# Second MLP product from two fp16 halves, and the work of the slot shared anew between GpSimd, ScalarE and VectorE

## Chip, cores, metric

One core of a Trainium2 chip. The time is that of one execution on the device, in microseconds (us); three runs of each kernel are taken and the median is quoted.

## What is computed

The input x has 4 sequences of 2048 rows of 256 numbers, fp32. Two sublayers are applied, each wrapped as x + layernorm(f(layernorm(x))). Only the second is touched by the change; its f has two layers:

```python
x = x + layernorm(attn(layernorm(x)))            # softmax over the columns, one head
x = x + layernorm(ffn(layernorm(x)))
# ffn: two layers, each
h = shift_token(x)                               # right half of a row comes from the row before
q, k, v = split(h @ wqkv, 3)                     # 8 heads of 64
q, k = rotary(l2norm(q) * qs), rotary(l2norm(k) * ks)
x = x + local_attention(q, k, v) @ wo            # windows of 128 rows, own window and the one before
h = layernorm(shift_token(x)) * lg + lb
a, g = split(h @ w1 + b1, 2)                     # HID = 682 columns each
x = x + (a * gelu(g)) @ w2 + b2
```

## The kernel before

`phase_a` computes the first sublayer and stores its rows; `phase_b` computes the second. `phase_b` first prepares the weights in a block of its own (lines 519 to 646): it splits `wqkv`, `wo` and `w1` into a high and a low part, scales `w1` by a power of two so that both parts fit fp16, folds the scale of `w1` back through `w2` (L608), and scales the rotary tables (L578). This block ends when the slowest engine is done, and the pipeline starts after it.

The pipeline works on windows of 128 rows: 64 per layer, 128 in all. A **slot** `s` is one turn of every engine's `run(s, r, pairs, layer)`, with `r = s % 4`. The order of work on each engine is written out by hand in `run`, and engines meet at semaphores only; each engine runs its queue strictly in order. In slot `s`, TensorE does in turn: the transposes of q and k of window s-1 (L812, L819); the products of window s with `wqkv`, first q, then k, then v (L834), where v waits for `qT_lo`; the transposes of the attention weights of window s-2 (L850); its product with v (L862), which waits pair by pair for the copies `probsT` by ScalarE; the scores of window s-1 (L875); the product with `wo` (L888); the transpose of the next input (L801). Then comes the MLP, for two windows at a time: in an **even slot** the first MLP product, 66 fp16 matmuls (L909), in an **odd slot** the second, `hid` times `w2` in fp32 (L920), which also waits until three heads' scores have left bank 3. Every fourth slot the loop jumps back (`slots`), so every second even slot is the first after a jump.

The other engines in a slot:

- ScalarE: copies qT and kT (L939, L942); the squares of q and of k (L946, L948); the copy of v (L951); four copies `probsT` (L957); the copy oT (L960); eight exponentials (L967); the copy hT (L932); in even slots six gelus (L980). In an even slot the exp and gelu tables are loaded in turn.
- VectorE: qT_low and kT_low (L1063, L1065); in even slots `layer_output`, two additions (L1028); the statistics of the MLP input (L1072 to L1076, the last gives `var2`); the rotation of q in three products (L1006 to L1008); the normalised MLP input `xh` and its fp16 copy (L1082, L1085); the rotation of k; in odd slots of layer 2 the statistics of the output (L1035 to L1040); oT_low (L1055); the eight masked scores (L1103), with `ss_min` (L1015) ahead of the last pair; eight normalisations of the weights, with a reciprocal ahead of each pair (L1113, L1116), between them xp and hT_low; in odd slots of layer 2 the output's normalisation (L1049); in even slots six products `hid` (L1139).
- GpSimd: `rstd2` from `var2` (L1165); the sums of squares in six halvings (L1155), two of them here and four after qr; the low half of `xh` (L1170); the sums qr and kr (L1174, L1177); in odd slots of layer 2 `rstdf`; the power -1/2 of 16 norms, `rn` (L1188); k times its norm, `kr` (L1193); `xb` (L1199); in odd slots of layer 2 `fin` (L1205).
- SyncE starts the DMAs; each of its waits stands in front of what it queues later. The transposing DMA of `xh_hl` (L778) waits for `xh_hi` and `xh_lo`.

## Time and profile before

| | us |
|---|---|
| three runs | 3128.81, 3130.56, 3132.86 (median 3130.56) |
| the profiled execution | 3132.01 |
| its span in the trace | 3130.2 |
| phase A and the weights, until the pipeline starts | 0 to 722.8 |
| pipeline | 722.8 to 3130.2 |

In the text T is the start of an odd slot and U that of an even one, both counted from TensorE's first transpose of q (L812); "U+6.8" is 6.8 us after it. A busy time is the time in which at least one instruction of the group ran; matmuls overlap one another, so that starts, not durations, give their pace. A row's last bracket is the idle time of the engine just before it and what ended it. "Layer 1" and "layer 2" are the two layers of the second sublayer (`layer` 0 and 1 in the code).

### The profile page before, as it was taken

The page shows a single profiled execution, that of the slowest core. Times are in us where ns is not written, and L with a number is a line of the kernel's source. Part 1 is how long each engine was busy: PE and PEld are TensorE (multiplying, and loading weights), DVE is VectorE, ACT ScalarE, POOL GpSimd, SP SyncE. Part 2 cuts the span into 40 slices and gives each one's busy share as a digit, 9 for nine tenths or more (in the row PEclk, how much of TensorE's full clock was granted, in tenths as well). Part 3 has the DMA queues.
Part 4 walks back from the last instruction along what each step waited for, and adds up shares of the span by engine and source line. Part 5 has one row for each costly group of instructions (what it writes and reads, how often), then busy time and mean ns, then how long its engine had stood idle before and what let it go on. Part 6 is the DMA issues. An engine that isn't in the chain of part 4 may idle for free.

```text
span 3130.2 us, 79769 instructions
## 1 busy us (share of the span) xinstructions
...
## 2 busy tenths in 40 slices
...
DMA packets 273326, 177.65 MB, mean 57 GB/s; under 512 B 95758, under 2 KB 271090, under 8 KB 272754
## 3 DMA queue, kind: packets, MB, share of 16 engines
...
## 4 chain that ended last, share of the span: by engine, by line
PE 74%; POOL 1%; issue 1%; DVE 0%; ACT 0%; DMA 0%; POOLq 0%; SPq 0%; DVEq 0%; ACTq 0%
PE b_ps L834 17%; PE b_ps L909 15%; PE b_ps L920 10%; PE b_ps L862 8%; PE b_ps L850 7%; PE b_ps L888 6%; PE b_ps L875 6%; PE b_ps L819 2%; PE b_ps L812 2%; PE b_ps L801 1%; POOL b_sq L1155 0%; POOL b_rn L1188 0%; POOL b_t L1177 0%; POOL b_kr L1193 0%; DVE b_probs L1103 0%
## 5 line engine op out<-in xcount | busy, mean ns | idle before, releaser
L967 ACT ACTIVATE b_probs<-b_probs,b_negmax 128x256 f32<-128x256 f32 x1024 | 505.9, 496 | 78.3 <-DVE b_negmax L1103 77.4
L834 PE MATMUL b_ps<-b_wqkv,b_hT_hi 128*128 128x512 f32 x1536 | 494.6, 403 | 1.0 <-DVE b_hT_lo L991 1.0
L909 PE MATMUL b_ps<-b_h2T,b_w 128*128 128x256 f16 x4224 | 474.1, 273 | 6.4 <-DMA b_h2T<-b_xh_hl 6.4
L909 PEld LDWEIGHTS b_ps<-b_h2T,b_w 128*128 128x128 f16 x4224 | 414.3, 98 | 55.2 <-DMA b_h2T<-b_xh_hl 6.8
L1155 POOL TENSOR_TENSOR b_sq<-b_sq 128x512 f32<-128x512 f32 (+5 forms) x768 | 418.9, 545 | 64.8 <-ACT b_sq L948 24.7
L1188 POOL TENSOR_TENSOR b_rn<-b_ss_min,b_mhalf 128x16 f32<-128x16 f32 x128 | 377.4, 2949 | 109.9 <-DVE b_ss_min L1015 109.7
L1116 DVE TENSOR_SCALAR b_probs<-b_probs,b_rinv 128x256 f32<-128x256 f32 x1024 | 409.6, 442 | 18.2
L1165 POOL TENSOR_TENSOR b_rstd<-b_var,b_mhalf 128x1 f32<-128x1 f32 x128 | 72.1, 564 | 552.0 <-DVE b_var L1076 552.0
L417 PE MATMUL a_ps<-a_xn_hl,a_E 128*128 128x256 f16 x3072 | 344.5, 273 | 8.8 <-DVE a_E L293 8.8
L920 PE MATMUL b_ps<-b_w,b_hid 128*128 128x256 f32 x1536 | 342.2, 379 | 1.2 <-DVE b_hid L1139 1.2
L417 PEld LDWEIGHTS a_ps<-a_xn_hl,a_E 128*128 128x128 f16 x3072 | 299.4, 98 | 44.2 <-ACT a_e L366 9.6
L834 PEld LDWEIGHTS b_ps<-b_wqkv,b_hT_hi 128*128 128x128 f32 x1536 | 284.8, 192 | 55.2 <-ACT b_hT_hi L932 1.4
L1103 DVE CUSTOM_DVE_ANT_0 b_probs<-b_ps,b_mask,b_rn 128x256 f32<-128x256 f32 x768 | 324.5, 479 | 0.0
L920 PEld LDWEIGHTS b_ps<-b_w,b_hid 128*128 128x128 f32 x1536 | 286.8, 190 | 37.9 <-DVE b_hid L1139 1.5
L834 PE MATMUL b_ps<-b_wqkv,b_hT_lo 128*128 128x512 f32 x768 | 304.6, 397 | 0.0
L957 ACT COPY b_probsT<-b_ps 128x512 f32<-128x512 f32 x512 | 264.0, 610 | 4.7 <-PE b_ps L850 4.6
L980 ACT ACTIVATE b_gl<-b_ps,b_b,b_w_unit 128x256 f32<-128x256 f32 (+1 forms) x384 | 203.1, 562 | 101.3 <-DVE b_hid L1139 69.1
L862 PE MATMUL b_ps<-b_probsT,b_v 128*64 128x128 f32 x4096 | 251.9, 276 | 0.0
L850 PEld LDWEIGHTS b_ps<-b_ident_f,b_probs 128*128 128x128 f32 x2048 | 232.7, 142 | 20.0 <-DVE b_xpp L1028 2.5
L850 PE MATMUL b_ps<-b_ident_f,b_probs 128*128 128x128 f32 x2048 | 245.9, 273 | 3.5 <-DVE b_xpp L1028 2.2
L862 PEld LDWEIGHTS b_ps<-b_probsT,b_v 128*64 128x64 f32 x4096 | 220.9, 137 | 21.5 <-ACT b_probsT L957 18.1
L1139 DVE SCALAR_TENSOR_TENSOR b_hid<-b_ps,b_b1a,b_gl 128x256 f32<-128x256 f32 (+1 forms) x384 | 177.0, 478 | 53.2 <-ACT b_gl L980 46.7
...
## 6 DMA issues: line engine op xcount, KB each, us to landing
b_hx<-xs_dram SPq DMA_DIRECT2D x256, 64.0 KB, 1.9
b_rot<-rot_dram SPq DMA_DIRECT2D x128, 128.0 KB, 2.1
b_xr<-xs_dram SPq DMA_DIRECT2D x128, 128.0 KB, 2.1
xp_dram<-b_xp SPq DMA_DIRECT2D x128, 128.0 KB, 1.7
b_h<-xp_dram SPq DMA_DIRECT2D x256, 64.0 KB, 1.8
...
```

Of the source, the lines that this page charges most:

```text
L417: last = nc.tensor.matmul(ps[:, bank, 0:D], E[:, j, a, i * P:(i + 1) * P], xn_hl[:, b % 2, j, c, :], start=(j == 0 and a == 0 and c == 0), ...
L834: last = nc.tensor.matmul(ps[:, bank, :], hT[:, k, :], wqkv[:, ds(layer(s), 1), part, k, bank * INNER:(bank + 1) * INNER], start=(k == 0 a ...
L850: last = nc.tensor.transpose(ps[:, 3 + p, n * P:(n + 1) * P], probs[:, 2 * p + n // 2, (n % 2) * P:(n % 2 + 1) * P], ident_f[:])
L862: last = nc.tensor.matmul(ps[h * DH:(h + 1) * DH, 7, p * P:(p + 1) * P], v[:, window, (2 * p + h) * DH:(2 * p + h + 1) * DH], probsT[:, p, ...
L909: last = nc.tensor.matmul(ps[:, bank, half * 2 * P:(half + 1) * 2 * P], w1[:, ds(layer(2 * j), 1), wp, k, first:first + P], h2T[:, hp, k, ...
L920: last = nc.tensor.matmul(ps[:, 3, n * D:(n + 1) * D], hid[:, c, n * P:(n + 1) * P], w2[:, ds(layer(2 * j), 1), c, :], start=(c == 0), sto ...
L957: nc.scalar.copy(probsT[:, p, :], ps[:, 3 + p, :]).then_inc(pT_kept, 1)
L967: nc.scalar.activation(probs[:, h, :], probs[:, h, :], ACT.Exp, bias=negmax[:, h:h + 1], scale=-1.0, accum_out=rowsum[:, h:h + 1]).then_in ...
L1103: nc.vector.tensor_tensor_reduce(probs[:, h, :], head_scores(h), which, rn[:, (r - 1) % 2, h:h + 1], ABOVE_ALL, ALU.add, ALU.min, negmax[: ...
L1116: nc.vector.tensor_scalar(probs[:, h, :], probs[:, h, :], rinv[:, h:h + 1], None, ALU.mult).then_inc(probs_ready, 1)
L1155: nc.gpsimd.tensor_tensor(target, target, sq[:, :, width:2 * width], ALU.add).then_inc(ss_halved, 1)
L1188: nc.gpsimd.tensor_tensor(rn[:, r % 2, :], ss_min[:], mhalf[:], ALU.pow).then_inc(rn_ready, 1)
```

## The change

In the steady part, the second MLP product takes three fp16 products (high by high, high by low, low by high) in place of one fp32 product; GpSimd splits `hid` into the halves `hid_hl`, four of the six blocks at the end of an even slot and two in the odd slot behind `rstd2` and `shift2`. Its unit is restored in `layer_output`. ScalarE makes `xh` and its fp16 copy from `rstd2` and a new `shift2`, between the squares and `probsT`, and copies v behind `probsT`. The sum of squares is one halving on GpSimd and a reduction on VectorE (`sum_squares`), which stands ahead of the output's statistics. The norms of k and of q are raised to the power apart, k's first. A rotation is two products, and one reciprocal serves four heads. The semaphore counts follow (three terms become two).

```diff
@@ ... steady part
-        pe.wait_ge(hid_ready, HC * (j + 1))
+        pe.wait_ge(hid_lo, HC * (j + 1))
         if in_range(s - 1):
             pe.wait_ge(scores_kept, HEADS * (s - 1) + BANK_READ[3])
         for n in range(2):
             for c in range(HC):
-                last = nc.tensor.matmul(ps[:, 3, n * D:(n + 1) * D], hid[:, c, n * P:(n + 1) * P], w2[:, ds(layer(2 * j), 1), c, :],
-                                        start=(c == 0), stop=(c == HC - 1))
+                for a, (hp, wp) in enumerate(PARTS):
+                    last = nc.tensor.matmul(ps[:, 3, n * D:(n + 1) * D], hid_hl[:, hp, c, n * P:(n + 1) * P],
+                                            w2[:, ds(layer(2 * j), 1), wp, c, :],
+                                            start=(c == 0 and a == 0), stop=(c == HC - 1 and a == 2))
         last.then_inc(w2_done, 1)
...
-        act.wait_ge(v_done, s + 1)
-        wait(act, pv_done, s - 2)
-        nc.scalar.copy(v[:, r, :], ps[:, 2, :]).then_inc(v_kept, 1)
+    t = s - 3
+    if in_range(t):
+        act.wait_ge(shift2_ready, t + 1)
+        wait(act, xh_lo, t)
+        nc.scalar.activation(xh[:], h2[:, (r - 3) % 2, :], ACT.Identity, bias=shift2[:], scale=rstd2[:]).then_inc(xh_ready, 1)
+        wait(act, h2T_loaded, 16 * t)
+        nc.scalar.activation(xh_hl[:, 0, :], h2[:, (r - 3) % 2, :], ACT.Identity, bias=shift2[:], scale=rstd2[:]).then_inc(xh_hi, 1)
     t = s - 2
     if in_range(t):
         wait(act, pv_done, t)
         for p in range(HP):
             act.wait_ge(pT_done, HP * t + p + 1)
             nc.scalar.copy(probsT[:, p, :], ps[:, 3 + p, :]).then_inc(pT_kept, 1)
+    if in_range(s):
+        act.wait_ge(v_done, s + 1)
+        wait(act, pv_done, s - 2)
+        nc.scalar.copy(v[:, r, :], ps[:, 2, :]).then_inc(v_kept, 1)
+    if in_range(t):
         act.wait_ge(pv_done, t + 1)
         wait(act, wo_done, t)
+        nc.vector.tensor_tensor(by_half(t2[:, n, :]), by_half(ps[:, n, :])[:, :, ::-1, :],
+                                factor(2 * n + 1).rearrange("p h (c d) -> p h c d", c=2), ALU.mult).then_inc(terms, 1)
...
         wait(dve, rn_ready, s)
-        nc.vector.tensor_scalar(ss_min[:], sq[:, :, 0], 1e-24, None, ALU.max).then_inc(ss_ready, 1)
+        nc.vector.tensor_scalar(ss_min[:], ss[:], 1e-24, None, ALU.max).then_inc(ss_ready, 1)
+def sum_squares(s):
+    if in_range(s):
...
+        nc.vector.tensor_reduce(ss[:], sq[:, :, 0:DH // 2], AX.X, ALU.add).then_inc(ss_summed, 1)
+def norm_stats(s, r):
+    t = s - 3
+    if in_range(t):
+        dve.wait_ge(h2_loaded, 32 * (t + 1))
+        nc.vector.bn_stats(st2[:], h2[:, (r - 3) % 2, :]).then_inc(st2_ready, 1)
+        wait(dve, shift2_ready, t)
+        wait_apart(dve, st2_ready, t + 1, passed_dve)
+        nc.vector.bn_aggr(mv2[:], st2[:]).then_inc(mv2_ready, 1)
+        dve.wait_ge(mv2_ready, t + 1)
+        nc.vector.tensor_scalar(var2[:], mv2[:, 1:2], EPS, None, ALU.add).then_inc(var2_ready, 1)
+        nc.vector.tensor_scalar(negmean2[:], mv2[:, 0:1], -1.0, None, ALU.mult).then_inc(negmean2_ready, 1)
 def layer_output(j, r, layer):
...
+                                           ALU.mult, ALU.add).then_inc(xpp_ready, 1)
 def output_stats(j, r, layer):
...
     layer_output(pairs - 3, r, layer)
...
-        wait_apart(dve, st2_ready, t + 1, passed_dve)
-        nc.vector.bn_aggr(mv2[:], st2[:]).then_inc(mv2_ready, 1)
-        dve.wait_ge(mv2_ready, t + 1)
-        nc.vector.tensor_scalar(var2[:], mv2[:, 1:2], EPS, None, ALU.add).then_inc(var2_ready, 1)
+    norm_stats(s, r)
     rotate(s, r, 0, q_sq, q_terms, qr_ready)
-    t = s - 3
-    if in_range(t):
-        dve.wait_ge(rstd2_ready, t + 1)
-        wait(dve, xh_lo, t)
-        nc.vector.tensor_scalar(xh[:], h2[:, (r - 3) % 2, :], mv2[:, 0:1], rstd2[:], ALU.subtract, ALU.mult).then_inc(xh_ready, 1)
-        dve.wait_ge(xh_ready, t + 1)
-        wait(dve, h2T_loaded, 16 * t)
-        nc.vector.tensor_copy(xh_hl[:, 0, :], xh[:]).then_inc(xh_hi, 1)
     rotate(s, r, 1, k_sq, k_terms, kr_ready)
+    sum_squares(s)
     output_stats(pairs - 3, r, layer)
...
-            nc.vector.reciprocal(rinv[:, 2 * p:2 * p + 2], rowsum[:, 2 * p:2 * p + 2]).then_inc(rinv_ready, 1)
-            dve.wait_ge(rinv_ready, HP * t + p + 1)
+            if p % 2 == 0:
+                dve.wait_ge(exp_done, HEADS * t + 2 * p + 4)
+                nc.vector.reciprocal(rinv[:, 2 * p:2 * p + 4], rowsum[:, 2 * p:2 * p + 4]).then_inc(rinv_ready, 1)
+                dve.wait_ge(rinv_ready, 2 * t + p // 2 + 1)
...
+        wait(dve, hid_lo, HC * j)
...
-def halve(s, first, end):
-    if in_range(s):
-        pool.wait_ge(k_sq, s + 1)
-        for n in range(first, end):
-            width = DH >> (n + 1)
-            target = sq[:, :, 0:width]
-            wait(pool, ss_halved, HALVINGS * s + n)
-            nc.gpsimd.tensor_tensor(target, target, sq[:, :, width:2 * width], ALU.add).then_inc(ss_halved, 1)
+def hid_halves(j, first, end):
+    if in_range(2 * j):
+        wait(pool, w2_done, j)
+        for c in range(first, end):
+            rows = slice(0, P if c < FULL else REST)
+            wait_apart(pool, hid_ready, HC * j + c + 1, passed_pool)
+            nc.gpsimd.tensor_copy(hid_hl[rows, 0, c, :], hid[rows, c, :]).then_inc(hid_hi, 1)
+            pool.wait_ge(hid_hi, HC * j + c + 1)
+            nc.gpsimd.tensor_tensor(hid_hl[rows, 1, c, :], hid[rows, c, :], hid_hl[rows, 0, c, :], ALU.subtract).then_inc(hid_lo, 1)
...
     if in_range(t):
         pool.wait_ge(var2_ready, t + 1)
+        wait(pool, xh_hi, t)
         nc.gpsimd.tensor_tensor(rstd2[:], var2[:], mhalf[:, 0:1], ALU.pow).then_inc(rstd2_ready, 1)
-    halve(s, 0, 2)
-    if in_range(t):
+        pool.wait_ge(negmean2_ready, t + 1)
+        pool.wait_ge(rstd2_ready, t + 1)
+        nc.gpsimd.tensor_tensor(shift2[:], negmean2[:], rstd2[:], ALU.mult).then_inc(shift2_ready, 1)
+    if r % 2 == 1:
+        hid_halves(pairs - 2, HID_EARLY, HC)
+    if in_range(s):
+        pool.wait_ge(k_sq, s + 1)
+        nc.gpsimd.tensor_tensor(sq[:, :, 0:DH // 2], sq[:, :, 0:DH // 2], sq[:, :, DH // 2:DH], ALU.add).then_inc(ss_halved, 1)
+    t = s - 3
+    if in_range(t):
+        pool.wait_ge(xh_ready, t + 1)
         pool.wait_ge(xh_hi, t + 1)
         wait(pool, h2T_loaded, 16 * t)
         nc.gpsimd.tensor_tensor(xh_hl[:, 1, :], xh[:], xh_hl[:, 0, :], ALU.subtract).then_inc(xh_lo, 1)
     if in_range(s):
-        pool.wait_ge(q_terms, 3 * (s + 1))
+        pool.wait_ge(q_terms, 2 * (s + 1))
         wait(pool, qT_done, s)
         nc.gpsimd.tensor_tensor(qr[:], t1[:, 0, :], t2[:, 0, :], ALU.add).then_inc(qr_ready, 1)
-        halve(s, 2, HALVINGS)
-        pool.wait_ge(k_terms, 3 * (s + 1))
+        pool.wait_ge(k_terms, 2 * (s + 1))
         nc.gpsimd.tensor_tensor(t1[:, 1, :], t1[:, 1, :], t2[:, 1, :], ALU.add).then_inc(kr_sum, 1)
...
-        wait(pool, scores_kept, HEADS * (s - 1))
-        nc.gpsimd.tensor_tensor(rn[:, r % 2, :], ss_min[:], mhalf[:], ALU.pow).then_inc(rn_ready, 1)
-    if in_range(s):
-        pool.wait_ge(rn_ready, s + 1)
+        nc.gpsimd.tensor_tensor(rn_k[:], ss_min[:, HEADS:2 * HEADS], mhalf[:, 0:HEADS], ALU.pow).then_inc(rnk_ready, 1)
+        pool.wait_ge(rnk_ready, s + 1)
         pool.wait_ge(kr_sum, s + 1)
         wait(pool, kT_done, s)
         nc.gpsimd.tensor_tensor(by_head(kr[:]), by_head(t1[:, 1, :]),
-                                rn[:, r % 2, HEADS:2 * HEADS].unsqueeze(2).to_broadcast([P, HEADS, DH]), ALU.mult).then_inc(kr_ready, 1)
+                                rn_k[:].unsqueeze(2).to_broadcast([P, HEADS, DH]), ALU.mult).then_inc(kr_ready, 1)
+        wait(pool, scores_kept, HEADS * (s - 1))
+        nc.gpsimd.tensor_tensor(rn[:, r % 2, :], ss_min[:, 0:HEADS], mhalf[:, 0:HEADS], ALU.pow).then_inc(rn_ready, 1)
     t = s - 2
     if in_range(t):
         pool.wait_ge(xp_ready, t + 1)
         wait(pool, xpp_ready, t - 3)
         nc.gpsimd.tensor_tensor(xb[:, (r - 2) % 4, :], xp[:, r % 2, :], b2[:, ds(layer(t), 1), :], ALU.add).then_inc(xb_ready, 1)
```

While the weights are prepared, `w2` is scaled and split, the first columns of `w1` (those of a) take a scale that bounds `hid`, and the loads of `w2` and `b1` stand ahead of those of the rotary tables and `wqkv`; two reductions over the partitions stand where one was. The mask is loaded in three kinds in place of five. `load_hx`, `load_rot`, `phase_a` and the work of the other lines stay as they are.

```diff
@@ ... preparation
-        w2 = sb("w2", [P, LAYERS, HC, D])
+        w2 = sb("w2", [P, LAYERS, 2, HC, D], F16)
+        w2_unit = sb("w2_unit", [P, LAYERS])
...
+for l in range(LAYERS):
+    sp.dma_start(w2_f[:, l, 0:FULL, :], w["w2"][l, 0:FULL * P, :].rearrange("(c p) d -> p c d", p=P)).then_inc(loaded_mlp, 16)
+    for first_block, first_row, half in ((0, 0, 0), (HC, SECOND_REST, HID)):
...
-        nc.gpsimd.partition_all_reduce(top_all[:], top[:], P, RED_MAX).then_inc(top_shared, 1)
+        pool.wait_ge(top_ready, 4 * LAYERS)
+        nc.gpsimd.partition_all_reduce(top_all[:].rearrange("p n l -> p (n l)"), top[:].rearrange("p n l -> p (n l)"), P, RED_MAX).then_inc(top_shared, 1)
+        nc.gpsimd.partition_all_reduce(sq_all[:], top_sq[:], P, RED_ADD).then_inc(top_shared, 1)
...
+for l in range(LAYERS):
+    nc.scalar.activation(w2[:, l, 0], w2_f[:, l], ACT.Copy, scale=w2_scale[:, l:l + 1]).then_inc(w2_hi, 1)
...
+    dve.wait_ge(top_ready, l + 1)
+    nc.vector.tensor_tensor(top_sq[:, l:l + 1], top[:, 0, l:l + 1], top[:, 0, l:l + 1], ALU.mult)
...
+for l in range(LAYERS):
+    nc.vector.tensor_tensor(b1[:, l, :], ps[:, l, 0:W1_BLOCKS], b1_f[:, l, :], ALU.add).then_inc(bias_added, 1)
+    nc.vector.tensor_reduce(top[:, 2, l:l + 1], w2_f[:, l].rearrange("p c d -> p (c d)"), AX.X, ALU.max, apply_absolute_value=True).then_inc(top_ready, 1)
+for l in range(LAYERS):
+    dve.wait_ge(bias_added, l + 1)
+    nc.vector.tensor_reduce(top[:, 1, l:l + 1], b1[:, l, :], AX.X, ALU.max, apply_absolute_value=True).then_inc(top_ready, 1)
+    nc.vector.tensor_scalar(top_sq[:, l:l + 1], top_sq[:, l:l + 1], 2.0, None, ALU.mult).then_inc(top_ready, 1)
...
+nc.vector.tensor_tensor(w1a_scale[:], hid_scale[:], w1_scale[:], ALU.min).then_inc(scale_ready, 1)
+dve.wait_ge(scale_ready, 1)
+nc.vector.reciprocal(w1a_unit[:], w1a_scale[:]).then_inc(step, 1)
+dve.wait_ge(step, 13)
+nc.vector.tensor_tensor(w2_unit[:], w1a_unit[:], w2_low[:], ALU.mult)
...
+    for columns, by in ((slice(0, A_COLUMNS), w1a_scale), (slice(A_COLUMNS, W1_BLOCKS * P), w1_scale)):
+        nc.vector.scalar_tensor_tensor(w1[:, l, 1, :, columns], w1_f[:, l, :, columns], by[:, l:l + 1], w1[:, l, 0, :, columns],
+                                       ALU.mult, ALU.subtract)
...
+for l in range(LAYERS):
+    dve.wait_ge(w2_hi, l + 1)
+    nc.vector.scalar_tensor_tensor(w2[:, l, 1], w2_f[:, l], w2_scale[:, l:l + 1], w2[:, l, 0], ALU.mult, ALU.subtract)
```

## Rows read from the trace of the kernel before

**Rows 1.** Busy time in one odd and one even slot of layer 2, summed.
```profile
sum 36.59, PE 36.59 PEld 32.65 DVE 33.34 ACT 25.05 POOL 25.53; mean PE 18.30 PEld 16.33 DVE 16.67 ACT 12.52 POOL 12.77
```

**Rows 2.** Timeline of TensorE, layer 1, from an odd slot's last product: start, duration.
```profile
2001.61 5.34 PE L920 MATMUL b_ps<-b_w,b_hid 128*128 128x256 f32 x24
2006.79 0.60 PE L812 MATMUL b_ps<-b_ident_f,b_qr 128*128 128x128 f32 x4
...
2013.61 1.97 PE L862 MATMUL b_ps<-b_probsT,b_v 128*64 128x128 f32 x32
...
2018.86 7.37 PE L909 MATMUL b_ps<-b_h2T,b_w 128*128 128x256 f16 x66
2026.06 0.60 PE L812 MATMUL b_ps<-b_ident_f,b_qr 128*128 128x128 f32 x4
```

**Rows 3.** The page: all six forms of the halving on GpSimd.
```profile
L1155 POOL TENSOR_TENSOR b_sq<-b_sq 128x512 f32<-128x512 f32 (+5 forms) x768 | 418.9, 545 | 64.8 <-ACT b_sq L948 24.7
```

**Rows 4.** Groups by line and form: count, busy us, mean ns, idle before.
```profile
L1155 POOL TENSOR_TENSOR b_sq<-b_sq 128x512 f32<-128x512 f32 x128 | 164.4, 1285 | 24.7 <-ACT b_sq L948 24.7
...
L1170 POOL TENSOR_TENSOR b_xh_hl<-b_xh,b_xh_hl 128x256 f16<-128x256 f32 x128 | 86.4, 675 | 39.5 <-DVE b_xh_hl L1085 39.5
...
L1165 POOL TENSOR_TENSOR b_rstd<-b_var,b_mhalf 128x1 f32<-128x1 f32 x128 | 72.1, 564 | 552.0 <-DVE b_var L1076 552.0
...
L221 POOL TENSOR_TENSOR a_rstd_c<-a_pow_c,a_unscale 128x1 f32<-128x1 f32 x64 | 12.2, 190 | 5.0
...
L619 DVE TENSOR_REDUCE p_top<-p_w_f 128x1 f32<-128x2816 f32 x2 | 6.2, 3086 | 0.1
...
L1113 DVE RECIPROCAL b_rinv<-b_rowsum 128x2 f32<-128x2 f32 x512 | 80.1, 156 | 0.0
```

**Rows 5.** Timeline of GpSimd in the even slot of rows 2.
```profile
2019.52 3.02 POOL L1188 TENSOR_TENSOR b_rn<-b_ss_min,b_mhalf 128x16 f32<-128x16 f32 x1 [1.13 <-DVE b_ss_min L1015]
2022.62 1.04 POOL L1193 TENSOR_TENSOR b_kr<-b_t,b_rn 128x512 f32<-128x512 f32 x1
2023.62 0.77 POOL L1199 TENSOR_TENSOR b_xb<-b_xp,b_b 128x256 f32<-128x256 f32 x1
```

**Rows 6.** Lines by form again, the five copies of GpSimd whose input the trace has.
```profile
L1161 POOL COPY b_mask_now<-b_mask 128x256 bf16<-128x256 bf16 x5 | 2.2, 433 | 0.0
```

**Rows 7.** Timeline of VectorE, an odd slot of layer 2, then a slot behind a jump.
```profile
2615.28 0.15 DVE L1076 TENSOR_SCALAR b_var<-b_mv 128x1 f32<-128x1 f32 x1
...
2619.48 0.73 DVE L1035 BATCH_NORM_STATS2 b_stf<-b_xpp 128x6 f32<-128x256 f32 x2
...
2620.76 0.69 DVE L1055 TENSOR_TENSOR b_oT<-b_ps,b_oT 128x512 fp32r<-128x512 f32 x1
...
2628.99 0.73 DVE L1049 TENSOR_SCALAR b_fin<-b_xpp,b_mvf,b_rstdf 128x256 f32<-128x256 f32 x2
2630.94 0.69 DVE L1063 TENSOR_TENSOR b_qT_low<-b_ps,b_qT 128x512 fp32r<-128x512 f32 x1 [1.22 <-issue]
```

**Rows 8.** Timeline of VectorE, start of the same even slot.
```profile
2005.94 1.36 DVE L1116 TENSOR_SCALAR b_probs<-b_probs,b_rinv 128x256 f32<-128x256 f32 x2
2008.05 0.69 DVE L1063 TENSOR_TENSOR b_qT_low<-b_ps,b_qT 128x512 fp32r<-128x512 f32 x1 [0.75 <-ACT b_qT L939]
...
2010.70 0.15 DVE L1076 TENSOR_SCALAR b_var<-b_mv 128x1 f32<-128x1 f32 x1
```

**Rows 9.** Timeline of VectorE while the weights are prepared.
```profile
704.23 11.70 DVE L637 SCALAR_TENSOR_TENSOR b_w<-p_w_f,p_w_scale,b_w 128x2816 f16<-128x2816 f32 x1
...
716.99 3.14 DVE L637 SCALAR_TENSOR_TENSOR b_w<-p_w_f,p_w_scale,b_w 128x2816 f16<-128x2816 f32 x1
```

**Rows 10.** Timeline of ScalarE in the same even slot.
```profile
2012.46 2.05 ACT L957 COPY b_probsT<-b_ps 128x512 f32<-128x512 f32 x4
...
2019.84 0.49 ACT L967 ACTIVATE b_probs<-b_probs,b_negmax 128x256 f32<-128x256 f32 x1
```

**Rows 11.** Timeline of TensorE in the pipeline's second slot.
```profile
743.17 1.11 PE L819 MATMUL b_ps<-b_ident_f,b_kr 128*128 128x128 f32 x4 [6.18 <-POOL b_kr L1193]
```

More of the change, by code:

```diff
@@ L49 @@
 W1_TOP = 2.0 ** 13
+W2_TOP = 2.0 ** 13
+HID_TOP = 2.0 ** 14
+ROW_BOUND = 272.25
 NT = LAYERS * NW
@@ L678, in phase_b @@
             st2, mv2, var2, rstd2 = sb("st2", [P, 6]), sb("mv2", [P, 2]), sb("var2", [P, 1]), sb("rstd2", [P, 1])
+            negmean2, shift2 = sb("negmean2", [P, 1]), sb("shift2", [P, 1])
             xh, xh_hl = sb("xh", [P, D]), sb("xh_hl", [P, 2, D], F16)
@@ L828, in run @@
                             else:
-                                wait(pe, (q_terms, k_terms)[bank], 3 * s)
+                                wait(pe, (q_terms, k_terms)[bank], 2 * s)
                                 if r % 2 == 1:
@@ L901, in run @@
                             if bank < 2 and in_range(s):
-                                pe.wait_ge((q_terms, k_terms)[bank], 3 * (s + 1))
+                                pe.wait_ge((q_terms, k_terms)[bank], 2 * (s + 1))
                             if bank > 2 and in_range(s - 1):
```

136 lines of the change are left out of this document (72 added, 64 removed).

## The prediction

> **What bounds the kernel now.** I read the busy times of one pair of slots first. In an odd and an even slot of layer 2, 36.59 us together, TensorE has a matmul in flight for all of it, VectorE is busy for 33.34, GpSimd for 25.53, ScalarE for 25.05 [rows 1]. Then TensorE's timeline: its products follow one another without a gap, and the even slot that starts at 2006.79 lasts 19.27 us to 2026.06, the odd one of layer 2 17.28 (2611.29 to 2628.57, the edges of rows 1) [rows 2]. So the pipeline runs at TensorE's rate and the others have slack. The question is how little: VectorE has 3.3 us in 36.6, and every queue is in order, so what counts is when each engine comes to the one result that TensorE wants next.
>
> **The product.** The second MLP product starts at 2001.61 and its successor at 2006.79: 5.18 us for 12 fp32 products. The first MLP product, 66 fp16 matmuls of the same shape, takes from 2018.86 to 2026.06, 0.109 us each [rows 2]. The new product has 36 of them: 3.93 us. Per pair that removes 1.25 us, for 64 pairs **80 us**, if nothing else becomes late. An odd slot would last 16.03 us.
>
> **GpSimd.** It loses five of six halvings and gains the split of `hid`. The halvings cost 418.9/128 = 3.27 us a slot [rows 3], the one that stays 1.29 [rows 4]. One power over 16 columns takes 2.95 to 3.02 us [rows 5], over one 0.56 [rows 4]: 0.16 per column, so 1.7 over 8, and two of them 3.4. `shift2` costs 0.19, like the small product L221 [rows 4]. A block of `hid` is a copy and a subtraction. The subtraction has a row of its own form, the low half of `xh`, 0.675 us [rows 4]. The copy from fp32 to fp16 has none: the nearest is a copy of 256 bf16 at 0.43 [rows 6], the other bound a two-operand operation with 0.675; I take 0.43, since it too reads one tensor, and with the wait between the two 1.16 us a block, 1.4 at the other bound.
>
> The walk through an even slot: `ss_min` lets the power of k start at U+12.7 as before (2019.52), it ends at 14.4, `kr` (1.0) at 15.5, the power of q at 17.2, `xb` (0.8) at 18.0 [rows 5]; four blocks of `hid` then end at 22.6, which is T+3.4 of the odd slot. `kr` is 1.4 us earlier than before, more than the shorter slot asks. In the odd slot `var2` is there at T+4.14 now (2615.43) [rows 7] and some 0.4 earlier with fewer reciprocals, so GpSimd takes it at T+3.7, ends `shift2` at 4.5, two more blocks at 6.9 and the halving at 8.2.
>
> **VectorE.** It loses `xh` and its copy, one of three products in each rotation, and two reciprocals of 0.156 us, with their waits 0.38 a slot [rows 4]. It gains the reduction over 512 elements: 3.086 us for 2816 elements is 1.10 ns each [rows 4], so 0.6 us. The additions in `layer_output` gain a factor and `negmean2` is one more 0.15 operation as `var2` is [rows 8]: both lie before TensorE's next demand and I count nothing for them; they are 0.3 us of the range. What `xh` frees does not help by itself, because VectorE then waits for the halving: the reduction runs from T+8.2 to 8.9. In layer 1 the next operation, oT_low, starts at 9.5 anyway and nothing changes. In odd slots of layer 2 the output's statistics follow, 1.28 us (2619.48 to 2620.76), and oT_low starts at 10.2 in place of 9.47 [rows 7]: **D = 0.7 us late**, with it the scores, the normalisations and `fin`. Between oT_low (0.6 us) and `ss_min` at +12.7 lie six heads' scores, 0.41 each; so three have left bank 3 at T+12.0, and the product wants that at 12.1: no wait there.
>
> Whether the two engines hinder each other must be weighed. Two operations of the same form took 11.70 and 3.14 us, the first while GpSimd multiplied the rotary tables [rows 9], so the engines can hold each other up. I don't apply this to the reduction, which would otherwise cost up to 0.6 x 11.70/3.14 = 2.2 us and make D 2.3. The Trainium skill (GPSIMD Engine Reference, Key points) names as hit the VectorE instructions in a two-port mode or with two SBUF inputs, and the reduction has one input; no row here shows such a reduction beside GpSimd.
>
> **ScalarE, where I expect the change to be paid for.** `xh` and its fp16 copy now stand in ScalarE's queue ahead of `probsT`, and wait for `shift2`, which waits for `var2`. TensorE's product with v starts at U+6.82 (2013.61) and takes four pairs in 1.89 us [rows 2]. The four copies run from U+5.67 to 7.72 [rows 10]; the last is wanted at 6.82 + 3 x 0.47 = 8.2, so all may start 0.5 later, at U+6.2. From `var2` at V the chain is `rstd2` 0.56, `shift2` 0.19, three handovers of 0.08 (the gap between the power and `kr` in rows 5), then two activations, 0.45 each as two overlapping exponentials of 0.49 [rows 10]: the copies start at V+1.9. So **V may be U+4.3**, and each microsecond beyond it stops TensorE for one. Bounds for an activation of 256 columns are half and the whole of a copy of 512 (2.05/4 = 0.51) [rows 10]: V at 4.7 or 4.2.
>
> Now V in an even slot. In layer 1 VectorE is done with the slot before at U+0.51, starts qT_low at 1.26, behind ScalarE, and `var2` is ready at 4.06, 2.80 after that start [rows 8]. After the change the odd slot is 1.25 shorter and VectorE's tail 0.38: it is done at U+1.4, starts at 1.5, V = 4.3, and TensorE doesn't wait. Every fourth slot follows a jump of the loop, 14 times in layer 1 and 13 in layer 2; there VectorE needs 1.22 us between slots ("issue") [rows 7]: start at 2.6, V = 5.4, a stop of 1.1 us: **+15 us**. It costs nothing today, because it is hidden in the wait for ScalarE.
>
> In layer 2 `fin` ends at 2629.72, U+1.15 [rows 7]; it will be 1.15 + 1.25 - 0.38 + 0.7 = 2.7, start 2.8, V = 5.6: a stop of 1.3 us in 18 even slots, **+24 us**. Behind a jump V = 6.75, 2.4 us in 13 slots, **+32 us**.
>
> **Edits with one answer.** In odd slots V is below 4.3 and nothing stops. The copy of v ends by U+8.6, `wo` wants its bank at 10.3. SyncE's transposing DMA waits for `xh_lo` a microsecond longer than now, and the loads behind it in its queue wait for `xp` at T+15 anyway: nothing. Its output is wanted at U+12.
>
> **Ends.** Preparation: VectorE is the last engine there and gets two reductions over 1536 columns (1.7 us each), two low parts (3.14 x 1536/2816 = 1.7 each [rows 9]) and ten or so small operations (2 in all): **+9**, 5 to 16 with the loads that are moved ahead of `wqkv` and the second reduction over partitions. First slots: TensorE waits 6.18 us for `kr` in the second slot [rows 11], as long in the third, and 1.2 in the fourth. The chain loses 3.27 - 1.29 and 2.95 - 1.7, 3.3 us: 3.3 + 3.3 + 1.2, **-8**. Last slots: two activations and one block of `hid` in the open, **+1**.
>
> **Sum.** -80 + 15 + 24 + 32 + 9 - 8 + 1 = -7: 3125 for the profiled execution of 3132.0; that one lies 1.4 above the median 3130.6, so **3124**.
>
> **Rivals.**
> 1. TensorE stays the bound (chance 0.23). The stops above fall away if ScalarE's `xh` is done sooner or VectorE's tail is shorter than I have it; for it speaks that VectorE has less to do in every slot, against it that its order leaves the tail after the scores as long as it was. Time: 3132 - 80 + 9 - 8 + 1, less 1.4: 3053.
> 2. Slower: GpSimd's blocks cost 1.4 us in place of 1.16 (0.25). GpSimd is free at T+4.4, the halving ends at 9.5, D = 2.0. The product then waits 1.2 us for bank 3 in 32 odd slots of layer 2 (+38), oT_low of layer 1 is 0.7 late and moves V in 32 slots (+23), and odd slots stop for 0.13 (+8): 3193. It decides from where the second reduction ends beyond T+9.5 in layer 1, a copy of about 0.55 us. For it: every two-operand operation of GpSimd costs more than 0.6; against it: the copy of rows 6.
> 3. That the product is no cheaper than the fp32 one is excluded by the first product's rate in rows 2.
>
> **Numbers.** My own case has 0.52, with a range of 3100 to 3150: about half of it is faster, a quarter the same, a quarter slower, since 0.1 us on V moves the sum by 4 us and its bounds are 0.5 apart. A difference of 0.2% (6 us) is what can be told from none. Faster: 0.23 + 0.25 = 0.48; same 0.14; slower 0.13 + 0.25 = 0.38. The range runs to the other cases, 3055 to 3185, which leaves out the outer half of each.
>
> **What would show it.** Right: the second product at 0.11 us a matmul, 3.9 us in all; waits of TensorE before L862 on the `probsT` copies, of about 1.3 us in even slots of layer 2 and 2.4 behind a jump, one of 1.1 behind a jump in layer 1; odd slots of 16.0 us; VectorE idle at T+6 to 8 for the halving. Wrong: even slots of layer 2 at 19.3 us (rival 1); a wait of TensorE for the scores ahead of the second product, or copies on GpSimd at 0.6 us (rival 2); a preparation that ends more than 16 us later.

## The result, and the profile after

The changed kernel takes **3147.95 us** (median of five executions, 3145.26 to 3151.22) against 3130.56 (also five executions, 3128.81 to 3132.86): ratio 1.0058, 95% interval 1.0046 to 1.0070. It is slower by 0.6%, where the likeliest case was slightly faster; the time lies within the range.

From the page of the kernel after: busy time of each engine, then two groups of its products (busy, mean ns | idle before and what ended it).

```profile
PE 2915.6 (93%) x25720; PEld 2510.3 (80%) x25720; DVE 2500.4 (79%) x7203; ACT 2006.4 (64%) x4572; POOL 1974.8 (63%) x2468
...
L911 PE MATMUL b_ps<-b_probsT,b_v 128*64 128x128 f32 x4096 | 262.0, 281 | 27.8 <-ACT b_probsT L1013 26.3
...
L937 PE MATMUL b_ps<-b_wo,b_oT 128*128 128x256 f32 x1536 | 215.7, 289 | 39.2 <-DVE b_oT L1134 39.2
```

TensorE is no longer busy for the whole of a pair of slots. The windows of the same odd and even slot of layer 2 as [rows 1], the even one behind a jump of the loop (length, then busy time of TensorE, its weight loads, VectorE, ScalarE and GpSimd, granted clock, DMA share, GB/s):

```profile
2606.01:2623.47 17.46, 16.16 (x151) 14.34 (x150) 14.71 (x45) 12.77 (x32) 13.78 (x20) 1.00 0.11 31
2623.47:2644.49 21.02, 19.57 (x181) 17.06 (x180) 16.68 (x53) 14.44 (x35) 15.34 (x17) 1.00 0.26 76
```

TensorE is busy for 16.16 and 19.57 us, so it is idle for 1.30 and 1.45. The pair lasts 38.48 us in place of 36.59, at a granted clock of 1.00 in both. TensorE's waits of the run (us in all, times, longest) name the two results that it stands for:

```profile
PE b_ps L937 <- DVE b_oT L1134: 39.2, 30, 1.4
PE b_ps L911 <- ACT b_probsT L1013: 26.3, 40, 1.9
```

Slot by slot, from the starts of the transposes of q (L812, now L861), after less before, us: up to the first slot +11.05; first four slots -9.3; 32 or 33 slots each of layer 1, odd -39.3 (16.08 for 17.27) and even +11.9 (19.67 for 19.29); 29 each of layer 2, odd **+5.4** (17.46 for 17.27) and even +29.5 (20.31 for 19.30); last slots +6.6. Sum +15.9, the difference of the spans.

The new product is what it should be, and the wait is ahead of `wo`. TensorE in the odd slot T = 2606.01:

```profile
2617.79 1.69 PE L937 MATMUL b_ps<-b_wo,b_oT 128*128 128x256 f32 x12 [1.30 <-DVE b_oT L1134]
...
2619.54 4.09 PE L970 MATMUL b_ps<-b_w,b_hid_hl 128*128 128x256 f16 x36
2623.47 0.60 PE L861 MATMUL b_ps<-b_ident_f,b_qr 128*128 128x128 f32 x4
```

3.93 us from L970 to L861. Why oT_low (the low half of oT, which `wo` reads) is late, VectorE and then GpSimd in the same slot; in [rows 7] are their counterparts of before:

```profile
2614.04 0.69 DVE L1080 TENSOR_REDUCE b_ss<-b_sq 128x16 f32<-128x512 f32 x1 [1.96 <-POOL b_sq L1241]
2614.64 0.74 DVE L1114 BATCH_NORM_STATS2 b_stf<-b_xpp 128x6 f32<-128x256 f32 x2
2615.31 0.42 DVE L1117 BATCH_NORM_AGGREGATE b_mvf<-b_stf 128x2 f32<-128x6 f32 x2
2615.76 1.38 DVE L1119 TENSOR_SCALAR b_varf<-b_mvf 128x2 f32<-128x2 f32 x1
2617.05 0.68 DVE L1134 TENSOR_TENSOR b_oT<-b_ps,b_oT 128x512 fp32r<-128x512 f32 x1
```

```profile
2610.53 0.40 POOL L1219 CAST b_hid_hl<-b_hid 128x256 f16<-128x256 f32 x1
2611.01 0.68 POOL L1221 TENSOR_TENSOR b_hid_hl<-b_hid,b_hid_hl 128x256 f16<-128x256 f32 x1
2611.63 0.40 POOL L1219 CAST b_hid_hl<-b_hid 42x256 f16<-42x256 f32 x1
...
2612.73 1.28 POOL L1241 TENSOR_TENSOR b_sq<-b_sq 128x512 f32<-128x512 f32 x1
...
2614.60 1.29 POOL L1251 TENSOR_TENSOR b_qr<-b_t 128x512 f32<-128x512 f32 x1
2615.84 1.27 POOL L1253 TENSOR_TENSOR b_t<-b_t 128x512 f32<-128x512 f32 x1
```

The variance (`varf`, L1119: epsilon is added to two values per partition) lasts 1.38 us and ends with GpSimd's sum for k (L1253). oT_low starts at T+11.04; it was T+9.47.

In the even slot U = 2623.47 ScalarE stands for `shift2`, which waits for `var2`, and the copies of `probsT` stand behind it. VectorE, ScalarE and TensorE:

```profile
2629.04 0.15 DVE L1092 TENSOR_SCALAR b_var<-b_mv 128x1 f32<-128x1 f32 x1
...
2630.28 0.60 ACT L1005 ACTIVATE b_xh<-b_h,b_shift,b_rstd 128x256 f32<-128x256 f32 x1 [2.35 <-POOL b_shift L1235]
2630.79 0.59 ACT L1007 ACTIVATE b_xh_hl<-b_h,b_shift,b_rstd 128x256 f16<-128x256 f32 x1
2631.28 2.02 ACT L1013 COPY b_probsT<-b_ps 128x512 f32<-128x512 f32 x4
...
2631.90 2.12 PE L911 MATMUL b_ps<-b_probsT,b_v 128*64 128x128 f32 x32 [1.45 <-ACT b_probsT L1013]
```

### The profile page after: what moved, and what is told of

The parts are those of the page before. It is cut to its first block and busy times, and to the rows that moved or that the text cites. A ratio compares the mean times of both kernels' runs of the same rounds, so it can differ in the third digit from the quotient of the medians.

```text
span 3146.1 us, 81396 instructions
## 1 busy us (share of the span) xinstructions
PE 2915.6 (93%) x25720; PEld 2510.3 (80%) x25720; DVE 2500.4 (79%) x7203; ACT 2006.4 (64%) x4572; POOL 1974.8 (63%) x2468
## 5 line engine op out<-in xcount | busy, mean ns | idle before, releaser
L1263 POOL TENSOR_TENSOR b_rn_k<-b_ss_min,b_mhalf 128x8 f32<-128x8 f32 x128 | 226.1, 1767 | 335.4 <-DVE b_ss_min L1074 335.4
L1181 DVE TENSOR_SCALAR b_probs<-b_probs,b_rinv 128x256 f32<-128x256 f32 x1024 | 333.6, 378 | 9.0
L911 PE MATMUL b_ps<-b_probsT,b_v 128*64 128x128 f32 x4096 | 262.0, 281 | 27.8 <-ACT b_probsT L1013 26.3
L1221 POOL TENSOR_TENSOR b_hid_hl<-b_hid,b_hid_hl 128x256 f16<-128x256 f32 (+1 forms) x384 | 258.2, 672 | 30.7
L911 PEld LDWEIGHTS b_ps<-b_probsT,b_v 128*64 128x64 f32 x4096 | 219.1, 137 | 65.5 <-ACT b_probsT L1013 45.3
L970 PE MATMUL b_ps<-b_w,b_hid_hl 128*128 128x256 f16 x2304 | 263.3, 273 | 3.0 <-POOL b_hid_hl L1221 3.0
L937 PE MATMUL b_ps<-b_wo,b_oT 128*128 128x256 f32 x1536 | 215.7, 289 | 39.2 <-DVE b_oT L1134 39.2
L970 PEld LDWEIGHTS b_ps<-b_w,b_hid_hl 128*128 128x128 f16 x2304 | 225.6, 98 | 29.4 <-POOL b_hid_hl L1221 3.2
L1134 DVE TENSOR_TENSOR b_oT<-b_ps,b_oT 128x512 fp32r<-128x512 f32 x128 | 88.1, 689 | 189.8 <-ACT b_oT L1021 189.8
```

The costliest lines, as they stand in the source:

```text
L911: last = nc.tensor.matmul(ps[h * DH:(h + 1) * DH, 7, p * P:(p + 1) * P], v[:, window, (2 * p + h) * DH:(2 * p + h + 1) * DH], probsT[:, p, ...
L970: last = nc.tensor.matmul(ps[:, 3, n * D:(n + 1) * D], hid_hl[:, hp, c, n * P:(n + 1) * P], w2[:, ds(layer(2 * j), 1), wp, c, :], start=(c ...
L1181: nc.vector.tensor_scalar(probs[:, h, :], probs[:, h, :], rinv[:, h:h + 1], None, ALU.mult).then_inc(probs_ready, 1)
L1221: nc.gpsimd.tensor_tensor(hid_hl[rows, 1, c, :], hid[rows, c, :], hid_hl[rows, 0, c, :], ALU.subtract).then_inc(hid_lo, 1)
L1263: nc.gpsimd.tensor_tensor(rn_k[:], ss_min[:, HEADS:2 * HEADS], mhalf[:, 0:HEADS], ALU.pow).then_inc(rnk_ready, 1)
```

## The experiments

Slot lengths (odd and even slots of layer 1 and 2) are means over one profiled execution, from the starts of the transposes of q (L861 in the kernel after), with the slots at the ends of a layer left out; ratios are to the kernel before on the same chip. The experiments ran on several chips, so that kernels are compared best by their ratios.

| | odd 1 | even 1 | odd 2 | even 2 | us, median | ratio (95%) |
|---|---|---|---|---|---|---|
| before | 17.27 | 19.29 | 17.27 | 19.30 | 3130.6 | |
| after | 16.08 | 19.67 | 17.46 | 20.33 | 3148.0 | 1.0058 |
| statistics first† | 16.08 | 19.65 | 16.08 | 20.22 | 3100.9 | 0.9916 (0.9900-0.9931) |
| halving first | 16.08 | 19.64 | 17.46 | 20.44 | 3147.6 | 1.0057 (1.0043-1.0072) |
| wait for variance | 16.07 | 19.63 | 16.23 | 20.33 | 3109.0 | 0.9938 (0.9924-0.9952) |
| probsT first | 16.30 | 19.69 | 16.94 | 19.74 | 3116.7 | 0.9962 (0.9947-0.9976) |
| two probsT ahead* | 16.08 | 19.95 | 16.08 | 19.97 | 3103.0 | 0.9919 (0.9903-0.9936) |
| product in 32 bits | 17.33 | 19.50 | 17.33 | 19.55 | 3150.4 | 1.0072 (1.0055-1.0089) |
| VectorE normalises* | 16.08 | 19.35 | 17.81 | 19.35 | 3113.1 | 0.9949 (0.9932-0.9965) |
| rotary loads first* | 16.08 | 19.67 | 16.08 | 20.21 | 3097.6 | 0.9903 (0.9887-0.9920) |
| by parity‡ | 16.08 | 19.36 | 17.49 | 19.36 | 3062.4 | 0.9789 (0.9775-0.9803) |
| by parity, 32 bits | 17.33 | 19.35 | 17.33 | 19.35 | 3133.2 | 1.0013 (1.0004-1.0023) |
| variance on GpSimd | 16.08 | 19.66 | 16.08 | 20.40 | 3108.6 | 0.9939 (0.9925-0.9953) |
| by parity, variance on GpSimd | 16.08 | 19.35 | 16.08 | 19.35 | 3062.3 | 0.9783 (0.9769-0.9796) |

\* made on the kernel with the statistics first.

† Three executions, 3100.0 to 3105.8. A fourth took 3162.9 us and is left out; what lengthened it isn't known. The later expectations take 3103.3, the median of all four.

‡ The slot lengths are those of the one long execution (3096.4), the median is that of all six.

### Odd slots of layer 2: four runs on the late oT_low

**Statistics first.**

```diff
-                    sum_squares(s)
                     output_stats(pairs - 3, r, layer)
+                    sum_squares(s)
```

> VectorE takes the statistics of the output (1.3 us of work, in odd slots of layer 2 alone) ahead of its sum over the squares, where it now stands idle for GpSimd's halving; nothing else is changed. Theory A: in these 30 slots the reduction's end at T+8.7 is now followed by the four statistics, the last of which (the variance) lasts 1.38 us, so that oT_low starts at T+11.0 and TensorE's product with wo waits 1.3 us for it (39.2 us over the run). With the statistics first oT_low starts at T+8.8 to T+9.6, the odd slots of layer 2 fall from 17.46 to 16.1 us, and the kernel takes 3109 us (3100 to 3120). Rival B: the time of the odd slots is kept by something else (the halving behind the blocks of the split, or TensorE's own work), so that another wait takes the place of this one: 3140 to 3150. Rival C: the even slots give back what the odd ones gain, since their stop hangs on VectorE's chain and not on TensorE: 3120 to 3135.

3100.9 us; by the ratios 44 us less than after. Theory A. TensorE's wait for oT_low is gone. The variance still lasts 1.00 us in the median, but it now lies in time in which VectorE would wait for the halving.

**Halving first.** In `run` of GpSimd the call of `hid_halves` for the last two blocks goes behind the halving.

> GpSimd halves the squares ahead of the two last blocks of the split, instead of behind them; nothing else is changed. Theory A: the halving starts when k's squares are there (T+4.5) and ends at T+5.8 instead of T+8.0, the reduction follows the rotations at once, the statistics end before T+9.5, the 39 us of TensorE's waits for oT_low go, and the kernel takes 3109 us (3100 to 3120), as with the statistics first. The two blocks end by T+8.5, far ahead of the product. Rival B: the delay has nothing to do with where the blocks stand, but comes from the variance alone (1.38 us instead of 0.2), which meets GpSimd's work wherever it stands: less than half of the gain, 3130 to 3145.

3147.6 us, no gain at all: theory A fell, and the time lies above B's range too, though B named the cause. VectorE was 2.06 us earlier at the variance (T+7.69 for T+9.75), and lost all of it there. Its timeline, then GpSimd's:

```profile
2614.30 0.42 DVE L1117 BATCH_NORM_AGGREGATE b_mvf<-b_stf 128x2 f32<-128x6 f32 x2
2614.75 3.44 DVE L1119 TENSOR_SCALAR b_varf<-b_mvf 128x2 f32<-128x2 f32 x1
2618.11 0.68 DVE L1134 TENSOR_TENSOR b_oT<-b_ps,b_oT 128x512 fp32r<-128x512 f32 x1
```

```profile
2614.39 0.67 POOL L1221 TENSOR_TENSOR b_hid_hl<-b_hid,b_hid_hl 42x256 f16<-42x256 f32 x1
2615.02 0.67 POOL L1247 TENSOR_TENSOR b_xh_hl<-b_xh,b_xh_hl 128x256 f16<-128x256 f32 x1
2615.65 1.28 POOL L1251 TENSOR_TENSOR b_qr<-b_t 128x512 f32<-128x512 f32 x1
2616.90 1.26 POOL L1253 TENSOR_TENSOR b_t<-b_t 128x512 f32<-128x512 f32 x1
```

The variance didn't get in between any two of these four: it ended at 2618.19, when GpSimd's row of instructions did (2618.16).

**Wait for the variance.** GpSimd, ahead of its sum for k in odd slots of layer 2:

```diff
                         pool.wait_ge(k_terms, 2 * (s + 1))
+                        if r % 2 == 1 and in_range(2 * j) and layer(2 * j) == 1:
+                            pool.wait_ge(varf_ready, j - NW // 2 + 1)
```

> One wait more, and nothing less: in odd slots of layer 2 GpSimd starts the sum of k's two terms only once VectorE has written the variances of the output. Theory A, the hold-up: the variance, a tensor_scalar of 2 values, lasts 1.38 us because GpSimd's sum (1.27 us) runs beside it and ends with it; it takes 0.15 to 0.25 us where GpSimd stands still. Then the added wait makes oT_low 1.1 to 1.2 us earlier in 30 slots and the kernel takes 3113 us (3108 to 3122), while GpSimd's sum is later by 0.1 to 0.2 us, which is covered. Rival B: the variance waits for something that the record doesn't tell (the statistics' own results), and GpSimd's sum only happens to end with it: the wait costs nothing or delays k, 3147 to 3155.

3109.0 us, in A's range. A wait more makes the kernel 39 us faster: it leaves a gap of 0.12 us between GpSimd's two sums. The variance over the run in the kernel after, then in this one (min/median/max in ns):

```profile
L1119 DVE TENSOR_SCALAR b_varf<-b_mvf x32: 170/1386/1400, 2010.9 to 3140.4; 128x2 f32<-128x2 f32 x32
```

```profile
L1119 DVE TENSOR_SCALAR b_varf<-b_mvf x32: 169/169/170, 2009.0 to 3098.8; 128x2 f32<-128x2 f32 x32
```

Rival B, that it waited for the results of the statistics, is out: they are the same in both.

**Variance on GpSimd.** The `tensor_scalar` leaves VectorE; GpSimd adds epsilon right before its power, by a `tensor_tensor` with a constant.

> The changed kernel, in which VectorE no longer writes the variance of the output: GpSimd adds the epsilon itself, right before its power. All else stays, the statistics behind the reduction and the blocks ahead of the halving too. Theory A: of VectorE's instructions between the halving and oT_low only this tensor_scalar within SBUF is held by GpSimd; the reduction, the statistics and oT_low (which reads PSUM) keep their durations of 0.69, 0.74, 0.42 and 0.69 us beside GpSimd's sums. oT_low starts at T+9.7 to T+9.9, the odd slots of layer 2 fall from 17.46 to 16.1 us: 3109 us (3104 to 3116). Rival B: the hold-up passes to the next instruction, oT_low: 3135 to 3150.

3108.6 us, odd slots at 16.08: the hold-up didn't pass to another instruction. Three edits that share only this, that the variance no longer stands unguarded ahead of oT_low, give 37 to 44 us each by the ratios: this cause is shown. Why GpSimd's instructions hold the variance is not.

### Even slots: where the normalisation stands

**probsT first.** ScalarE's copies of `probsT` go ahead of its two activations.

> ScalarE copies probsT ahead of its two normalisations instead of behind them; nothing else is changed. Theory A: the stop of TensorE in the even slots (1.45 us behind a loop jump of layer 2, 0.3 us in layer 1) is ScalarE's wait for shift2 ahead of probsT. It goes: even slots fall by 0.4 us in layer 1 and 1.0 us in layer 2, together -41 us, 3107 us (3100 to 3118). Rival B: the normalised input of the MLP is now 1 us later, its transposition by DMA lands at U+13.5 to U+14.5, where W1's first product wants it at U+12.5, so that TensorE waits there instead: 3130 to 3150. Odd slots keep their length under both.

3116.7: within A's range, but not by A's account, for even slots of layer 1 kept their length (19.69) and odd ones grew. The stop before L911 went, but two others came: the weight loads of the first MLP product wait 0.32 us on average in 54 slots, and with two activations more ahead of oT's copy odd slots last 16.30 in layer 1. The row of the first names no engine ("issue"); that it is the transposed input, as B had it, is read from one slot, where its DMA is issued at 1424.04, takes 2.4 us to land, and the first load starts at 1426.60:

```profile
PEld b_ps L958 <- issue: 17.3, 54, 1.8
```

In layer 2 the odd slots are mixed, 16.3 or 17.36: the variance took 0.17 us in 14 of 32 and 1.25 to 1.30 in the others.

**Two probsT ahead**, in even slots only.

> Stands on the kernel with the statistics first (3103.3 us). In even slots ScalarE copies the first two heads' pairs of probsT ahead of the two normalisations and the other two behind them; in odd slots the order stays. Theory A: the stop of TensorE in the even slots is the wait of probsT behind shift2. With all four copies ahead the stop went, but TensorE then waited 0.3 us in each even slot for the transposed input of the MLP, and oT was 0.2 us late in odd slots. With two ahead the input is 1 us earlier than there and in time, and the third copy comes at U+7.9 behind a loop jump, 0.4 to 0.7 us late: even slots of layer 1 fall from 19.65 to 19.3 us, those of layer 2 from 19.7 to 19.3 and from 21.0 to 19.9: -32 us, 3071 us (3066 to 3085). Rival B: what lengthens the even slots of layer 1 by 0.35 us is not this stop (they kept 19.64 us with all copies ahead): only layer 2 gains, 3080 to 3092. Rival C: the transposed input is late again: 3090 to 3103.

No gain (the ratios are 0.9919 and 0.9916). The time lies at the edge of C's range, but no rival had the cause: the third copy now follows two copies and two activations and is late in every even slot, 19.95 and 19.97 us, by ScalarE's own work (it runs from U+5.72 on without a gap) and no longer by `shift2`.

```profile
PEld b_ps L911 <- ACT b_probsT L1007: 52.2, 170, 0.7
```

**VectorE normalises.** As before the change, between its rotations.

> Stands on the kernel with the statistics first (3103.3 us). The input of the MLP is normalised by VectorE between its two rotations, as before the change, and no longer by ScalarE; the shift on GpSimd goes. Theory A: with it the wait ahead of probsT leaves ScalarE's queue, the even slots fall back to 19.3 us (-11 us in layer 1, -31 in layer 2), and VectorE's 0.7 us more is covered by its idle time ahead of oT_low: 3062 us (3058 to 3075). Rival B: the two added instructions of VectorE (a tensor_scalar and a copy within SBUF) are of the kind that GpSimd holds up; with the blocks of the split and the halving beside them they last 1 to 2 us instead of 0.2 to 0.4, the rotation of k and the reduction come later, and k's chain or oT_low makes TensorE wait in odd slots: 3080 to 3140.

3113.1. A was right in the even slots: they are 19.35 us in both layers, so all but 0.05 us of their +0.38 and +1.03 hung on the normalisation in ScalarE's queue. B was right in the time and in that odd slots pay, not in the instruction: the two that were added last 0.64 and 0.33 us in odd slots of layer 2 (medians). They move the variance to T+8.07, there it lasts 2.74 us, and the reduction stands behind it:

```profile
2593.27 2.74 DVE L1110 TENSOR_SCALAR b_varf<-b_mvf 128x2 f32<-128x2 f32 x1
2595.93 0.68 DVE L1073 TENSOR_REDUCE b_ss<-b_sq 128x16 f32<-128x512 f32 x1
2596.52 0.68 DVE L1125 TENSOR_TENSOR b_oT<-b_ps,b_oT 128x512 fp32r<-128x512 f32 x1
```

### What the product itself is worth

**Product in 32 bits**, all else as changed.

> The changed kernel with the second product of the MLP in 32 bits as before: no split of the hidden values, no blocks on GpSimd; all other parts of the change stay, the statistics behind the reduction among them. Theory A: the 16-bit product is worth 1.25 us in every odd slot in place, and the blocks on GpSimd cost nothing in layer 1; in layer 2 oT_low is late because the variance is held by GpSimd's unbroken row of instructions, blocks or none. The kernel takes 3148 + 80 = 3228 us (3218 to 3236), the odd slots 17.3 us in layer 1 and 18.7 us in layer 2, and TensorE still waits 1.3 us for oT_low. Rival B: the two blocks ahead of the halving are what makes oT_low late; without them the wait of 39 us goes: 3185 to 3195, odd slots 17.3 us in both layers.

3150.4, hardly slower than with 16 bits (by the ratios 4 us, and the intervals overlap): B's account holds in layer 2, but both ranges were missed. In layer 1 the product costs 17.33 - 16.08 = 1.25 us in each odd slot, as forecast; but without GpSimd's blocks the variance takes 0.17 us in all 32 slots, at T+7.7, and even slots are 0.17 and 0.78 us shorter. Within this change the blocks ate nearly all that the product gave.

**By parity, in 32 bits and in 16.** The statistics and the rotary loads first; VectorE normalises in even slots, between its rotations (the lines behind the "..."), ScalarE in odd ones (the lines ahead of it).

```diff
-                    if in_range(t):
+                    if r % 2 == 1 and in_range(t):
...
+                    if r % 2 == 0 and in_range(t):
+                        dve.wait_ge(rstd2_ready, t + 1)
+                        wait(dve, xh_lo, t)
+                        nc.vector.tensor_scalar(xh[:], h2[:, (r - 3) % 2, :], mv2[:, 0:1], rstd2[:], ALU.subtract, ALU.mult).then_inc(xh_ready, 1)
```

> Three edits to the changed kernel: the statistics of the output ahead of the reduction, the loads of the rotary table and the head scales ahead of those of w2 and b1, and the normalisation by the slot's parity: VectorE between its rotations in even slots, ScalarE in odd slots. Theory A: each slot has the shorter of the lengths measured so far, 16.08 us in odd slots of both layers (ScalarE normalises, the variance is held but covered) and 19.35 us in even slots (VectorE normalises, no wait ahead of probsT). Against 3103.3 us: 32 even slots of layer 1 by 0.31 and 28 of layer 2 by 0.87 less, 34 us, and 6 us from the loads: 3063 us (3058 to 3075). Rival B: the two orders disturb each other where they meet (a slot's values are normalised on one engine, the next slot's on the other, and xh is shared): one of the parities keeps its longer length, 3075 to 3100.

> The kernel by parity with the second product in 32 bits: no split, no blocks on GpSimd. Theory A: the 16-bit product is worth its full 1.25 us in 64 slots once nothing else is late; what it gained beside the rest of the change was nothing (3150.4 us in 32 bits, 3147.6 us in 16) only because its blocks on GpSimd lengthened waits that this kernel no longer has. 3063 + 80 - 3 (preparation) = 3140 us (3134 to 3147), odd slots 17.33 us, even slots 19.3 to 19.4 us. Rival B: with the blocks gone the even slots are shorter too, and the product is worth 60 us or less: 3110 to 3125.

3062.4 and 3133.2, the first as A had it, the second just below its 3134: here the same product is worth 71 us. The first slot starts 3.5 us later with it; where the rest of the 80 us goes isn't shown. One execution of six, the profiled one, took 3096.4. In its trace the variance lasts 0.99 to 1.02 us in 13 slots and 4.03 in 16, at the same place beside the same instructions, and TensorE waits for oT_low:

```profile
L1119 DVE TENSOR_SCALAR b_varf<-b_mvf x32: 169/2521/4033, 1991.2 to 3088.8; 128x2 f32<-128x2 f32 x32
PE b_ps L937 <- DVE b_oT L1134: 31.7, 17, 1.9
```

**By parity, variance on GpSimd.**

> The kernel by parity (3062.4 us; one execution of six, the profiled one, took 3096.4 us), in which GpSimd adds the epsilon to the output's variance, as in the run on that alone. Theory A: what made the one execution 34 us longer is the hold-up of the variance again: it lasted up to 4.03 us there, its end fell behind the reduction, and TensorE waited 31.7 us for oT_low in 17 odd slots of layer 2. Without this instruction on VectorE every execution, the profiled one too, has odd slots of 16.08 us in both layers: 3060 us (3055 to 3066), none above 3070. Rival B: the two tensor_scalars and the copy that VectorE now has in even slots, or oT_low itself, are held instead: single executions of 3080 to 3100 us remain.

3062.3 (3058.9 to 3065.4), the profiled one with a span of 3060.5 and every slot counted at its short length. None of five executions is long; since only one of six was, five don't show that none can be. It beats the kernel before by 2.2% and the changed one by 2.7% (0.9783/1.0058).

### Preparation

**Rotary loads first.**

> Stands on the kernel with the statistics first (3103.3 us). SP issues the loads of the rotary table and of the head scales ahead of the loads of w2 and b1 instead of behind them; nothing else is changed. Theory A: most of the 11 us by which the preparation grew is GpSimd's first multiplication of the table, which now starts at 689.3 us instead of 681.9 and holds VectorE's square of the largest weight for 8.15 us until it ends at 698.1. It starts 7 us earlier, VectorE is free 5 to 7 us earlier: 3097 us (3094 to 3100). Rival B: w2 and b1 then land later, and the largest of w2, the scales and everything behind them wait for these loads: 3102 to 3108.

3097.6, by the ratios 4 us less than with the statistics first; the first slot starts 4.5 us earlier. In the kernel after, VectorE's square of one value per partition was held until GpSimd's multiplication of the tables ended (689.26 to 698.07):

```profile
689.93 8.15 DVE L637 TENSOR_TENSOR p_top_sq<-p_top 128x1 f32<-128x1 f32 x1
```

With the loads first the square takes 0.16 us, but two larger `tensor_scalar`s, 1.82 us together in the kernel after, now take 6.29 beside the multiplication: the hold-up is shorter, not gone.

```profile
684.54 6.29 DVE L633 TENSOR_SCALAR p_w_f<-p_w_f,p_lg 128x1408 f32<-128x1408 f32 x2 [4.19 <-PE b_ps L606]
```

## Why the prediction was wrong

**Right, by its own steps.** The product takes 3.93 us as forecast, odd slots of layer 1 last 16.08 for 16.03. GpSimd: blocks at a pace of 1.10 us for 1.16, the power over 8 columns 1.77 for 1.7, the halving done at T+8.0 for T+8.2. The reduction 0.69 for 0.6, beside GpSimd's work. ScalarE's new wait stops TensorE in even slots, as the mechanism said. The preparation took +11 for +9, the first slots -9.3 for -8.

**The step that failed is D.** The prediction had VectorE's statistics at their old 1.28 us and oT_low at T+10.2. They took 2.41, because the variance is held for 1.2 us, and oT_low came at T+11.04: D was 1.57, not 0.7. The hold-up had been weighed, with [rows 9], and then asked of one instruction only, the reduction, which was not hit. It should have been asked of every VectorE instruction beside GpSimd's new work. The Trainium skill (SBUF — State Buffer, SBUF: two separate sides) has a pair of ports that GpSimd shares with VectorE instructions in a two-port mode or with two SBUF inputs, and that goes to whichever instruction starts first, for the whole of it. If the variance is of that kind, which the trace doesn't tell, it would wait for the sum under way, 0.1 us at 2615.76. The trace has more: it missed the handover there, and three of them in the run with the halving first.

**And D's first consumer was missed.** The text looked at bank 3 at T+12.1. But TensorE wants oT_low itself ahead of that, for `wo`, at T+10.48 (2617.79 - 1.30 - 2606.01). It starts 0.74 us after oT_low does; at T+9.47 that left 0.27 us, and 1.57 - 0.27 is the 1.30 us of the trace. At the forecast D of 0.7 this wait would have been 0.4, some 12 us over the 29 slots, for which the sum had nothing. The odd slots of layer 2 should have given -36 us and gave +5: **41 us**, more than what separates forecast and result (3124, 3148).

**Too dear were the even slots:** forecast 15 + 24 + 32 = 71, measured 11.9 + 29.5 = 41. The rule held, that each microsecond of V (the end of `var2`) stops TensorE for one, but its bound was U+4.05 and not 4.3: slots with V at 4.16, 4.64 and 5.72 last 19.38, 19.85 and 21.02 us, V + 15.2 or 15.3 each, and the slot before the change was 19.30. From V to the copies it is 2.09 us in the slot shown, not 1.9, with activations 0.50 apart for 0.45.

V itself came earlier than forecast. In layer 2 behind a jump it was U+5.72, not 6.75, because `fin` ended at U+1.66, not 2.7: from oT_low to the end of `fin` VectorE takes 8.08 us in place of 8.96, 0.88 less where 0.38 was forecast, and TensorE's wait of 1.30 us made U itself later. In layer 1 there was no stop of 1.1 us behind jumps. VectorE starts qT_low at U+1.25 to 1.34 in all 32 even slots, behind ScalarE, and V is U+4.16 to 4.64 in all. That is above the bound for two small reasons which the sum had at nothing, the factor in `layer_output` (0.87 us for 0.75) and, in some slots, the load of h2; the slot U = 1409.87 has the longest such wait:

```profile
1412.40 0.87 DVE L1106 SCALAR_TENSOR_TENSOR b_xpp<-b_ps,b_w_unit,b_xb 128x256 f32<-128x256 f32 x2
1413.58 0.43 DVE L1087 BATCH_NORM_STATS2 b_st<-b_h 128x6 f32<-128x256 f32 x1 [0.30 <-DMA b_h<-xp_dram]
```

So there are two errors of 41 and -30 us, and it is luck, by their opposite signs, that the time is only 24 us from the forecast. The last slots took +6.6 us (69.7 - 63.1) for +1. That is not put down to the change: from the start of the last transposes of q to the end, the kernels with the statistics first and with the rotary loads first, alike in this stretch, took 70.9 and 65.2 us.

**Of the rivals**, the first (3053) names what the best version reaches, by other means than it gave. The second had the right direction, a D well above 0.7 and a slower kernel, from a wrong cause: the blocks were cheaper than thought, not dearer, and TensorE waited ahead of `wo`, not for bank 3.
